# A perceiver layer on one core: the gate product taken in two halves of the tokens, and the threshold search moved ahead

## The chip, the cores and the metric

One core of a Trainium2 chip runs the whole kernel. Its five engines work side by side, each through its own queue in the order written: TensorE (PE, with its weight loads as PEld), VectorE (DVE), ScalarE (ACT), GpSimd (POOL) and SyncE (SP), which here only issues DMA transfers. They meet through semaphores. The metric is the time of one execution in microseconds, the median of several runs. Less is better.

## What is computed

Three residual blocks follow each other on 1024 tokens of width 1024: attention over 16 contexts, a gated feed-forward block whose gate is cut to half, and a mixture of low-rank experts. The change lies in the second.

```python
s = jax.nn.silu(jnp.einsum('bsh,ih->bsi', x, w_gate))       # I = 2752 columns
k = int(0.5 * I)
_, idx = jax.lax.top_k(-jnp.abs(s), k)                      # the k smallest of each row
flat = flat.at[rows, idx.reshape(B * S, k)].set(0.0)        # are set to zero
s = s * jnp.einsum('bsh,ih->bsi', x, w_up)
return jnp.einsum('bsi,hi->bsh', s, w_down)
```

## The kernel before

The tokens are 8 tiles of 128. After attention come four stages, in the function `fast`, which writes the program of every engine out by hand; what an engine does next is what its program says next, and tables of slot numbers put the search beside the products.

**Gate.** The weights come in 8 chunks of 344 columns (`NCH`, `NJ`). SP loads a chunk into the one buffer `g_raw` (1376 KB), POOL rounds it to `g_hi` (L1130) and subtracts to `g_lo` (L1132), and PE multiplies it by all 8 tiles, 24 matmuls each (L1842): the token side is split into `z_hi` and `z_lo` as well. Both halves of the weights have two buffers. Among the first products PE turns the tiles of z (L1825, `turn_z(t+1)` ahead of the product with tile t). ACT rounds them from banks 4 and 5 (L1586), DVE takes their low part (L1236) and normalises the tile after next. ACT takes each product out of one of six banks through Silu into `res` (L1607), and SP stores a chunk to the tensor `s` in memory. `res` lies in the space that the search uses later.

**Search.** For each row the kernel looks for the threshold below which half of |s| lies, on two tiles at a time (a pair). `measure` takes the magnitude of a loaded row tile `mag` and its sum (ACT, L1611). `guess` makes a first cut (DVE, L1268). Then come 7 rounds: DVE counts what lies below the cut in the pair's first tile (L1279), ACT in its second (`compare`, L1617), and DVE works a new cut out of both in eight to ten instructions on two numbers (L1286 to L1308). The seventh round counts both tiles on DVE. Then each tile is finished on DVE by `nearest` (L1316), `best` (L1322), `choose` (L1327 to L1343) and `keep` (L1349), which writes `sx`. SP stores that to `sk` and loads the next `sx` and `mag`. There are three buffers of `mag` and one of `sx`. The semaphore `kept` counts finished tiles.

**Up.** 44 products of 24 matmuls (L1866) run over 22 slices of `w_up_t` (`u_raw`, two buffers, split by POOL in L1139 and L1141); ACT copies each out (L1647), SP stores it to `u_t`. Pairs 0 and 1 are searched whole beside it, and the rounds of pair 2. `ABS_AT`, `ROUNDS_AT`, `MAG_AT` and `SK_AT` name the slots.

**Down.** 66 steps: three groups of tiles (0 to 2, 3 to 5, 6 and 7) times 22 slices. A step turns a slice of `sk` (PE, L1880), multiplies it by `t_u` (DVE, L1374), rounds it (ACT, L1665), takes the low part (DVE `take_low`, L1383), and makes 18 or 12 matmuls (L1897) with slices of `w_down` that POOL splits (L1151, L1153). DVE also finishes tiles 4 to 7 in steps 0 to 7 and 24 to 31 (`FINISH_AT`) and runs the rounds of pair 3 in steps 9 to 21 (`LATE_ROUNDS_AT`).

## Time and profile before

| | us |
|---|---|
| median of 3 runs | 1511.86 (1511.83 to 1512.56) |
| the profiled execution | 1506.71 |
| its span in the trace | 1504.5 |
| gate, up, down of tiles 0 to 5: start in the trace | 607.5, 860.4, 1107.0 |
| steps 44 to 65 of down and the last mixture: start | 1361.0 |

PE is busy for 93% of the span, DVE 67%, POOL 59%, ACT 46%. The mean clock granted to PE is 0.976 of full speed. The span is what the trace's windows add up to; the profiled execution is 2.2 us longer than it.

### The profile page before, as it was taken

How to read it: one execution, taken by the hardware profiler on the slowest of the kernel's cores; microseconds unless marked ns; L12 is line 12 of the kernel's file. 1: busy time of each engine (PE TensorE's matmuls, PEld its weight loads, DVE VectorE, ACT ScalarE, POOL GpSimd, SP SyncE). 2: the span in 40 equal slices, each digit the busy share in tenths (PEclk: the TensorE clock that was granted, in tenths of full speed). 3: DMA queues.
4: the chain of work that ended last, by engine and by line, in shares of the span. 5: the costliest groups of instructions: out<-in, count | busy, mean ns of one | idle time of the engine just before them, and what ended most of it. 6: DMA issues, size and time to landing. Idle time of an engine off the chain costs nothing.

```text
span 1504.5 us, 30249 instructions
## 1 busy us (share of the span) xinstructions
PE 1399.6 (93%) x12775; PEld 1029.4 (68%) x12775; DVE 1010.9 (67%) x1328; ACT 696.8 (46%) x905; POOL 880.8 (59%) x424
## 2 busy tenths in 40 slices
PE   3999999999999999899999999999987888899965
PEld 3555555555555555799999988888865666787843
DVE  7788888888888888810000059897558888655663
ACT  1788888888888888311111152424312320111211
POOL 0699888889888888332242123353245665687830
PEclk9999999999999999999999999999999998999987
DMA  9023433323232330023322373848277756855612
GB/s 334 2 89 108 151 107 129 104 90 103 89 103 90 103 104 2 29 76 109 117 76 76 99 253 94 299 151 284 78 256 263 263 154 215 275 170 172 179 50 86
DMA packets 110320, 208.04 MB, mean 138 GB/s; under 512 B 8080, under 2 KB 83936, under 8 KB 106080
## 3 DMA queue, kind: packets, MB, share of 16 engines
q1 hardware_dynamic: 89072, 183.47, 35.8%
q10 hardware_dynamic: 21104, 22.55, 4.9%
q8 instruction: 102, 1.67, 0.4%
q14 instruction: 42, 0.34, 0.1%
HBM read 163.80 MB, written 42.21 MB: 137 GB/s over the span
## 4 chain that ended last, share of the span: by engine, by line
PE 83%; DVE 10%; issue 4%; ACT 1%; DMA 1%; POOL 0%; DVEq 0%; ACTq 0%; SPq 0%; POOLq 0%
PE fast_psum L1866 16%; PE fast_psum L1842 16%; PE fast_psum L1759 15%; PE fast_psum L1777 14%; PE fast_psum L1897 10%; PE fast_psum L1796 5%; DVE fast_h_lo L1383 2%; PE fast_psum L1803 1%; PE fast_psum L1959 1%; PE fast_psum L1924 1%; PE fast_psum L1782 1%; DVE fast_ln_stats L98 1%; DVE fast_below L1279 1%; PE fast_psum L1880 1%; DMA fast_sx<-s 1%
## 5 line engine op out<-in xcount | busy, mean ns | idle before, releaser
L1209 DVE TENSOR_TENSOR fast_masked<-fast_psum,fast_mask_t 128x1024 f32<-128x1024 f32 (+1 forms) x416 | 488.1, 1218 | 68.7 <-PE fast_psum L1759 67.1
L1098 POOL TENSOR_TENSOR fast_pair<-fast_probs 128x1024 f32<-128x1024 f32 x192 | 457.2, 2384 | 107.4 <-ACT fast_probs L1549 49.2
L1549 ACT ACTIVATE fast_probs<-fast_masked 128x1024 f32<-128x1024 f32 (+1 forms) x416 | 437.5, 1058 | 64.7 <-DVE fast_masked L1209 49.9
L1759 PE MATMUL fast_psum<-fast_qT,fast_kraw 32*128 32x256 f32 (+1 forms) x3328 | 247.3, 403 | 1.5 <-DVE fast_masked L1209 0.8
L1777 PE MATMUL fast_psum<-fast_probs,fast_vraw 128*32 128x256 f32 (+1 forms) x3328 | 226.4, 386 | 0.8 <-ACT fast_probs L1549 0.8
L1759 PEld LDWEIGHTS fast_psum<-fast_qT,fast_kraw 32*128 32x128 f32 (+1 forms) x3328 | 154.1, 182 | 88.5 <-DVE fast_masked L1209 54.8
L1153 POOL TENSOR_TENSOR fast_d_lo<-fast_d_raw,fast_d_hi 128x1024 fp32r<-128x1024 f32 x66 | 164.1, 2487 | 5.3
L1842 PE MATMUL fast_psum<-fast_g_hi,fast_z_hi 128*128 128x344 f32 x512 | 164.8, 322 | 2.6 <-ACT fast_res L1607 2.6
L1842 PE MATMUL fast_psum<-fast_g_lo,fast_z_hi 128*128 128x344 f32 x512 | 163.7, 320 | 0.0
L1842 PE MATMUL fast_psum<-fast_g_hi,fast_z_lo 128*128 128x344 f32 x512 | 163.6, 320 | 0.0
L1268 DVE TENSOR_SCALAR fast_cut<-fast_total 128x2 f32<-128x2 f32 x4 | 0.7, 165 | 239.8 <-ACT fast_mag L1611 239.7
L1777 PEld LDWEIGHTS fast_psum<-fast_probs,fast_vraw 128*32 128x32 f32 (+1 forms) x3328 | 87.1, 109 | 107.0 <-ACT fast_probs L1549 47.5
L1897 PE MATMUL fast_psum<-fast_d_hi,fast_h_hi 128*128 128x512 f32 (+1 forms) x352 | 122.2, 430 | 38.5 <-DVE fast_h_lo L1383 30.1
L1665 ACT CAST fast_h_hi<-fast_t_h 128x384 fp32r<-128x384 f32 (+1 forms) x66 | 31.5, 477 | 266.0 <-DVE fast_t_h L1374 266.0
L1151 POOL CAST fast_d_hi<-fast_d_raw 128x1024 fp32r<-128x1024 f32 x66 | 73.6, 1114 | 119.8 <-PE fast_psum L1897 99.0
L1866 PE MATMUL fast_psum<-fast_z_hi,fast_u_hi 128*128 128x512 f32 (+1 forms) x352 | 139.3, 396 | 0.5 <-ACT fast_res L1607 0.5
L1866 PE MATMUL fast_psum<-fast_z_hi,fast_u_lo 128*128 128x512 f32 (+1 forms) x352 | 139.2, 395 | 0.0
L1866 PE MATMUL fast_psum<-fast_z_lo,fast_u_hi 128*128 128x512 f32 (+1 forms) x352 | 139.2, 395 | 0.0
L1139 POOL CAST fast_u_hi<-fast_u_raw 128x1024 fp32r<-128x1024 f32 (+1 forms) x22 | 25.1, 1142 | 183.1 <-PE fast_psum L1866 102.7
L1796 PE MATMUL fast_psum<-fast_pair,fast_ones 128*32 128x256 f32 x1536 | 118.1, 379 | 1.3 <-POOL fast_pair L1098 1.3
L1607 ACT ACTIVATE fast_res<-fast_psum 128x344 f32<-128x344 f32 x64 | 28.8, 459 | 192.1 <-PE fast_psum L1842 192.1
L1897 PE MATMUL fast_psum<-fast_d_lo,fast_h_hi 128*128 128x512 f32 (+1 forms) x352 | 115.2, 410 | 0.0
(150 smaller groups left out, 2020.5 us busy)
## 6 DMA issues: line engine op xcount, KB each, us to landing
fast_d_raw<-w_down SPq DMA_DIRECT2D x63, 512.0 KB, 3.8
fast_kraw<-ctx_t SPq DMA_DIRECT2D x32, 800.5 KB, 5.9
fast_vraw<-ctx_nat SPq DMA_DIRECT2D x16, 1536.0 KB
fast_g_raw<-w_gate SPq DMA_DIRECT2D x8, 1376.0 KB, 10.3
s<-fast_res SPq DMA_DIRECT2D x8, 1376.0 KB, 6.1
fast_mag<-s SPq DMA_DIRECT2D x8, 1376.0 KB, 10.1
fast_sx<-s SPq DMA_DIRECT2D x8, 1376.0 KB, 6.6
sk<-fast_sx SPq DMA_DIRECT2D x8, 1376.0 KB, 5.4
```

Of the source, the lines that this page charges most:

```text
L1098: pool.tensor_tensor(pair[:, n % PAIR_BUFS], both[:, :, 0, :], both[:, :, 1, :], ALU.add).then_inc(paired, 1)
L1151: pool.tensor_copy(d_hi[j][0:r, :], d_raw[j][0:r, :]).then_inc(d_hi_done, 1)
L1153: pool.tensor_tensor(d_lo[j][0:r, :], d_raw[j][0:r, :], d_hi[j][0:r, :].bitcast(F32), ALU.subtract).then_inc(d_lo_done, 1)
L1209: dve.tensor_tensor(into, of, m, ALU.add).then_inc(mask_added, 1)
L1549: act.activation(probs[0:r, g % RING, hp * HALF:(hp + 1) * HALF], masked[0:r, h % SLOTS, :], ACT.Exp).then_inc(exp_done, 1)
L1665: act.copy(h_hi[n % HS][0:r, 0:w], t_h[n % 2][0:r, 0:w]).then_inc(h_hi_done, 1)
L1759: last = pe.matmul(scores[0:r, (2 * g + hp) % SLOTS, h % 2, i * 256:(i + 1) * 256], kraw[b % BUFS][q, u, c * P:c * P + r], qT[q, b, u, :], ...
L1777: last = pe.matmul(o_acc[q, u, 0:256], vraw[b % BUFS][0:r, c, u * P + h * HD:u * P + (h + 1) * HD], probs[0:r, g % RING, (2 * h + i) * 256 ...
L1796: last = pe.matmul(o_acc[h * HD:(h + 1) * HD, u, 256:512], ones[:, :], pair[:, n % PAIR_BUFS, h, :], start=False, stop=final, skip_group_c ...
L1842: last = pe.matmul(bank[GATE_BANKS[i % GBANKS]][:, 0:NJ], zp[:, k, ts], wp[n % 2][:, k, :], start=(k == 0 and a == 0), stop=(k == DK - 1 a ...
L1866: last = pe.matmul(bank[i % 4][0:r, :], wp[f % 2][:, k, 0:r], zp[:, k, gs], start=(k == 0 and a == 0), stop=(k == DK - 1 and a == 2))
L1897: last = pe.matmul(bank[2 * i + o][:, :], hp[jh][0:r, ts], wp[j][0:r, o * 512:(o + 1) * 512], start=(k == 0 and a == 0), stop=(k == IC - 1 ...
```

## The change

The gate stage now runs over 16 chunks of 4 tiles: all 8 weight chunks with tiles 0 to 3, then the same 8 again with tiles 4 to 7. So each weight chunk is loaded and split twice. `g_raw` has two buffers; the high half is now rounded by ACT (`take_weights`) and only the low half is left to POOL. `res` is half as large and has moved, so the space of the search is free from the ninth chunk on. Pairs 0 and 1 are searched from slot 36 of the 64 gate slots, pairs 2 and 3 beside up, and nothing of the search is left in down.

```diff
+        HT = TILES // 2
+        CHUNKS = 2 * NCH
+        g_raw = [at("g_raw0", WEIGHTS, [DK, NJ]), at("g_raw1", THIN + 2 * HT * NJ, [DK, NJ])]
+        res = [at(f"res{j}", THIN + HT * NJ * j, [HT, NJ]) for j in range(2)]
-        ABS_AT = (0, 1, 13, 14, 27, 28, 38)
-        ROUNDS_AT = (2, 16, 30)
+        GATE_ABS_AT = {36: 0, 37: 1, 44: 2, 54: 3}
+        GATE_ROUNDS_AT = (38, 55)
+        UP_ABS_AT = {4: 4, 5: 5, 12: 6, 19: 7}
+        UP_ROUNDS_AT = (6, 20)
+        UP_SK_AT = {1: 2, 3: 3, 9: 4, 10: 5, 15: 6, 17: 7}
+        UP_MAG_AT = {0: 4, 1: 5, 3: 6, 9: 7}
-        FINISH_AT = {0: 4, 4: 5, 24: 6, 28: 7}
...
+            for c in range(CHUNKS):                       # SP
+                if c + 2 < CHUNKS:
+                    load_gate(c + 2)
...
+                store_gate(c)
+                if c + 1 == NCH:
+                    for j in range(2):
+                        sp.wait_ge(s_stored[j], 16 * (NCH // 2))
+                    for t in range(MAGS):
+                        load_mag(t)
+                    load_sx(0)
...
+            for c in range(1, CHUNKS):                    # POOL
+                j = c % 2
+                if c == 1:
+                    pool.wait_ge(z_ready, TILES)
+                    pool.wait_ge(pv_done, ASTEPS)
+                pool.wait_ge(g_hi_done, c + 1)
+                pool.tensor_tensor(g_lo[j][:, :, :], g_raw[raw(c)][:, :, :], g_hi[j][:, :, :].bitcast(F32),
+                                   ALU.subtract).then_inc(g_lo_done, 1)
...
+            for q in range(HT, SLOTS_G):                  # ACT
+                take_gate(q)
+                if q % HT == 0 and q // HT + 1 < CHUNKS:
+                    take_weights(q // HT + 1)
+                if q in GATE_ABS_AT:
+                    measure(GATE_ABS_AT[q])
+                for p in range(2):
+                    if 0 <= q - GATE_ROUNDS_AT[p] < ROUNDS - 1:
+                        compare(p, q - GATE_ROUNDS_AT[p])
...
+            for q in range(SLOTS_G):                      # PE
+                if q + 1 < TILES:
+                    turn_z(q + 1)
+                gate(q)
```

On ACT the products of a chunk stood in one row at the start of the gate. Before (`res0`, `res1` are the two halves of `res`, the CAST rows round tiles of z):

```order
L115 ACTIVATE fast_ln2_sd<-fast_ln2_mv 128x1
L1586 CAST fast_z_hi_61<-fast_psum 128x4x128 x2
L115 ACTIVATE fast_ln2_sd<-fast_ln2_mv 128x1
L1586 CAST fast_z_hi_61<-fast_psum 128x4x128 x4
L1607 ACT_TABLE_LOAD
L1607 ACTIVATE fast_res0_102<-fast_psum 128x344 x8
```

And after, from the same place of ACT:

```order
L1584 CAST fast_z_hi_61<-fast_psum 128x4x128 x2
L1601 CAST fast_g_hi1_66<-fast_g_raw0_63 128x2752
L115 ACTIVATE fast_ln2_sd<-fast_ln2_mv 128x1
L1584 CAST fast_z_hi_61<-fast_psum 128x4x128 x2
L115 ACTIVATE fast_ln2_sd<-fast_ln2_mv 128x1
L1584 CAST fast_z_hi_61<-fast_psum 128x4x128 x2
L115 ACTIVATE fast_ln2_sd<-fast_ln2_mv 128x1
L1584 CAST fast_z_hi_61<-fast_psum 128x4x128 x2
L1592 ACT_TABLE_LOAD
L1592 ACTIVATE fast_res0_103<-fast_psum 128x344 x4
L1584 CAST fast_z_hi_61<-fast_psum 128x4x128 x2
L1592 ACTIVATE fast_res1_104<-fast_psum 128x344
```

A rounding of weights stands among the tiles of z, and the last tile of z is taken after the first four products.

On SP, where the first half of the gate ends, after (before, the four loads of `mag` and `sx` stood behind the last store of the gate and a load of `u_raw`):

```order
L966 DMA s<-fast_res1_104 128x4x344
L985 DMA fast_mag0_105<-s 128x2752
L985 DMA fast_mag1_106<-s 128x2752
L985 DMA fast_mag2_107<-s 128x2752
L990 DMA fast_sx_111<-s 128x2752
L961 DMA fast_g_raw1_64<-w_gate 128x2752
L966 DMA s<-fast_res0_103 128x4x344
```

A load of gate weights now stands behind the four. 

On DVE, the first steps of down before (`t_h` is the product, `h_lo` its low part, the rest is the finishing of tile 4):

```order
L1374 TENSOR_TENSOR fast_t_h0_118<-fast_psum,fast_t_u0_114 128x384
L1316 SCALAR_TENSOR_TENSOR fast_near_107<-fast_mag1_105,fast_cut 128x2752
L1317 TENSOR_SCALAR fast_rank<-fast_off 128x1
L1374 TENSOR_TENSOR fast_t_h1_119<-fast_psum,fast_t_u1_115 128x384
L1383 TENSOR_TENSOR fast_h_lo0_123<-fast_t_h0_118,fast_h_hi0_120 128x384
L1322 MAX fast_top<-fast_near_107 128x8
L1374 TENSOR_TENSOR fast_t_h0_118<-fast_psum,fast_t_u2_116 128x384
```

And after:

```order
L1383 TENSOR_TENSOR fast_bad<-fast_bad,fast_outside 128x1
L1393 TENSOR_TENSOR fast_t_h0_119<-fast_psum,fast_t_u0_115 128x384
L1393 TENSOR_TENSOR fast_t_h1_120<-fast_psum,fast_t_u1_116 128x384
L1402 TENSOR_TENSOR fast_h_lo0_124<-fast_t_h0_119,fast_h_hi0_121 128x384
L1393 TENSOR_TENSOR fast_t_h0_119<-fast_psum,fast_t_u2_117 128x384
```

Only the steps' own products and low parts are left there.

## Rows read from the trace of the kernel before

**Rows 1.** The page's chain that ended last: share of the span by engine.
```profile
PE 83%; DVE 10%; issue 4%; ACT 1%; DMA 1%; POOL 0%; DVEq 0%; ACTq 0%; SPq 0%; POOLq 0%
```

**Rows 2.** Windows: stretch (us), length, each engine's busy us, PEclk, DMA share, GB/s.
```profile
640.00:860.40 220.40, 219.79 (x1393) 219.54 (x1393) 3.77 (x5) 28.23 (x63) 61.02 (x17) 0.99 0.26 89
860.40:1107.00 246.60, 246.60 (x1058) 196.19 (x1059) 174.87 (x301) 89.37 (x93) 81.07 (x44) 1.00 0.58 195
1107.00:1300.20 193.20, 156.63 (x660) 124.39 (x658) 170.66 (x214) 36.02 (x48) 113.67 (x63) 0.91 0.72 242
1300.20:1358.20 58.00, 58.00 (x272) 47.06 (x271) 26.24 (x50) 8.36 (x17) 47.15 (x26) 1.00 0.63 189
```

**Rows 3.** Waits of PE from 1107 to 1301: total, times, longest.
```profile
PE fast_psum L1897 <- DVE fast_h_lo L1383: 30.1, 12, 3.8
```

**Rows 4.** Chain in order of time, steps 21 to 23 of down: start, length, what.
```profile
1238.07 4.37 PE fast_psum L1897 x18
...
1245.37 6.90 PE fast_psum L1897 x18
...
1252.60 4.13 PE fast_psum L1897 x18
```

**Rows 5.** Timeline at the start of the gate, PE and POOL: start, length, instruction, [idle before].
```profile
627.14 1.04 PE L1825 MATMUL fast_psum<-fast_eye,fast_xres 128*128 128x128 f32 x8
...
633.87 2.49 POOL L1130 CAST fast_g_hi<-fast_g_raw 128x2752 fp32r<-128x2752 f32 x1 [22.07 <-DVE fast_xo L110]
636.43 6.03 POOL L1132 TENSOR_TENSOR fast_g_lo<-fast_g_raw,fast_g_hi 128x2752 fp32r<-128x2752 f32 x1
```

**Rows 6.** PE after a hole in the gate: timeline, and a window of that stretch.
```profile
640.06 0.63 PE L1842 MATMUL fast_psum<-fast_g_hi,fast_z_hi 128*128 128x344 f32 x1 [2.59 <-ACT fast_res L1607]
...
640.00:643.00 3.00, 2.94 (x10) 2.97 (x11) 2.97 (x2) 1.67 (x5) 2.47 (x1) 0.50 0.00 0
```

**Rows 7.** Timeline of ACT: a product taken out of the gate, a magnitude in up.
```profile
754.59 0.46 ACT L1607 ACTIVATE fast_res<-fast_psum 128x344 f32<-128x344 f32 x1 [3.30 <-PE fast_psum L1842]
...
877.10 2.51 ACT L1611 ACTIVATE fast_mag<-fast_mag 128x2752 f32<-128x2752 f32 x1 [0.25 <-DMA fast_mag<-s]
```

**Rows 8.** Transfers: SP and POOL timelines, and a DMA row (KB each, us to landing).
```profile
860.36 0.41 SPq L950 DMA_DIRECT2D s<-fast_res  x1
...
866.61 1.31 SPq L969 DMA_DIRECT2D fast_mag<-s  x3
...
888.23 1.04 POOL L1139 CAST fast_u_hi<-fast_u_raw 128x1024 fp32r<-128x1024 f32 x1 [12.72 <-DMA fast_u_raw<-w_up_t]
...
fast_g_raw<-w_gate SPq DMA_DIRECT2D x4, 1376.0 KB, 9.8
```

**Rows 9.** Timeline of DVE: meetings with POOL, a round, the finishing of a tile.
```profile
638.90 3.72 DVE L1251 TENSOR_SCALAR fast_inside<-fast_rden 128x256 f32<-128x256 f32 x1
...
889.38 2.38 DVE L1306 SCALAR_TENSOR_TENSOR fast_da<-fast_db,fast_da 128x2 f32<-128x2 f32 x1
...
899.01 3.08 DVE L1279 TENSOR_SCALAR_CACHE_REDUCE fast_below<-fast_mag,fast_cut 128x2752 bf16<-128x2752 f32 x1
...
903.89 3.08 DVE L1279 TENSOR_SCALAR_CACHE_REDUCE fast_below<-fast_mag,fast_cut 128x2752 bf16<-128x2752 f32 x1
...
938.92 3.08 DVE L1316 SCALAR_TENSOR_TENSOR fast_near<-fast_mag,fast_cut 128x2752 f32<-128x2752 f32 x1
...
949.95 3.08 DVE L1349 SCALAR_TENSOR_TENSOR fast_sx<-fast_near,fast_thr,fast_sx 128x2752 f32<-128x2752 f32 x1
```

**Rows 10.** Transfers of a finished tile and of up's weights: SP, POOL, a DMA row.
```profile
1028.65 0.32 SPq L978 DMA_DIRECT2D sk<-fast_sx  x1
1033.33 0.33 SPq L974 DMA_DIRECT2D fast_sx<-s  x1
...
1046.84 1.04 POOL L1139 CAST fast_u_hi<-fast_u_raw 128x1024 fp32r<-128x1024 f32 x1 [14.45 <-DMA fast_u_raw<-w_up_t]
...
fast_u_raw<-w_up_t SPq DMA_DIRECT2D x21, 512.0 KB, 6.9
```

More of the change, by code:

```diff
@@ L671, in fast @@
         PAIRS = TILES // 2
+        HT = TILES // 2
+        CHUNKS = 2 * NCH
+        SLOTS_G = CHUNKS * HT
         GROUPS = ((0, 1, 2), (3, 4, 5), (6, 7))
@@ L790, in fast @@
         z_lo_done = sem("z_lo_done")
-        g_full = sem("g_full")
+        g_full = [sem(f"g_full{j}") for j in range(2)]
         g_hi_done = sem("g_hi_done")
@@ L1351, in _ @@
             dve.wait_ge(iota_ready, 1)
-            for p in range(U_PAIRS):
+            for p in range(PAIRS):
                 guess(p)
@@ L1360, in _ @@
                     keep(t)
-            for r in range(ROUNDS):
-                if r == 0:
-                    guess(U_PAIRS)
-                search(U_PAIRS, r)
+            dve.wait_ge(step, steps[0])
+            done(dve.tensor_reduce(good[:, :], settled[:, :], AX.X, ALU.min))
+            dve.wait_ge(step, steps[0])
+            done(dve.tensor_scalar(bad[:, :], good[:, :], -1.0, 1.0, ALU.mult, ALU.add))
+            dve.wait_ge(step, steps[0])
+            dve.tensor_tensor(bad[:, :], bad[:, :], outside[:, :], ALU.add).then_inc(bad_ready, 1)
             def multiply(n):
@@ L1587, in take_z_high, with take_gate, take_weights @@
                          bank[4 + h].rearrange("p (k t) -> p k t", t=P)).then_inc(z_hi_done, 1)
+            def take_gate(q):
+                c, t = divmod(q, HT)
+                if t == 0 and c >= 2:
+                    act.wait_ge(s_stored[c % 2], 16 * (c // 2))
+                act.wait_ge(g_done, q + 1)
+                act.activation(res[c % 2][:, t, :], bank[GATE_BANKS[q % GBANKS]][:, 0:NJ], ACT.Silu).then_inc(g_copied, 1)
+            def take_weights(c):
+                act.wait_ge(g_full[raw(c)], 16 * raw_loads(c))
+                if c == 1:
+                    act.wait_ge(pv_done, ASTEPS)
+                    act.wait_ge(paired, B * (PER - 1))
+                else:
+                    act.wait_ge(g_done, (c - 1) * HT)
+                act.copy(g_hi[c % 2][:, :, :], g_raw[raw(c)][:, :, :]).then_inc(g_hi_done, 1)
             ln2.scalar(act, 0)
@@ L1594, in _ @@
             spread_output(UNITS - 1)
-            for t in range(1, TILES):
+            for t in range(1, TILES - 1):
                 if t + 1 < TILES:
```

168 lines of the change are left out of this document (62 added, 106 removed).

## Prediction

> **What bounds the kernel now.** I read the chain of work that ended last, then the windows by stage, then the waits of the stage that has holes, then the timeline of each engine around the places that the change touches. The chain is PE for 83% of the span and DVE for 10% [rows 1]: PE is the bound nearly everywhere. The windows say where not. In the gate after 640 us PE is busy 219.8 of 220.4 us, in up all of 246.6, in steps 31 to 43 of down all of 58.0. In steps 0 to 30 of down it is busy 156.6 of 193.2 us, at 0.91 of its clock, and DVE 170.7 [rows 2]. PE waits there for the low half that DVE makes, 12 times, 30.1 us in all [rows 3]: DVE has the search between its products. So the gate has nothing to win and everything to lose, and down has a gain with a ceiling.
>
> **What down gives back.** The 13 undisturbed steps take 58.0 us [rows 2], 4.46 each. Steps 0 to 30 at that pace are 138.3 us. The change of group at step 22 stays, since DVE there adds in the residual in both kernels: from the start of step 21 to that of step 23 there are 14.53 us where two steps are 8.92 [rows 4], so 5.6 is kept. Before step 0 the first slice must be turned, multiplied, rounded and subtracted in any case. I take 2.2 us for that, an estimate between nothing and the 5.6 of the change of group, where DVE has more to do. Sum 146.1 against 193.2: **47.1 us saved**. What is late next is PE itself; POOL keeps the pace of the 13 steps with DVE as empty as it will be now, since it is busy 47.2 of 58.0 us there [rows 2].
>
> **Its start costs the gate a hole.** The product with the second chunk was due after 8 tiles and is now due after 4: when PE has turned z tile 5, at 628.2 [rows 5]. Its low half still waits on POOL for all 8 tiles to be normalised, and POOL got that at 633.87 [rows 5]. The tile that comes last hangs on PE's turn at 627.14, which stands ahead of the product that waits, so it isn't late, but no earlier either. ACT has the high half ready before. POOL needs 6.1, so PE starts at 640.1: a hole of 11.9 us. After a hole PE runs at 0.50 of its clock, that is the 1.2 GHz level, for some microseconds [rows 6]; the step after 1245.37 took 6.90 instead of 4.37 [rows 4]. I take 2.3 for such a restart, between 0 and 2.5. Then a second hole: ACT takes z tile 6 after that product, loads its table, takes four products and z tile 7, and only then tile 4's product and chunk 2's weights (2.5, as a magnitude of the same width [rows 7]), then POOL's 6.1. By these lengths chunk 2 is ready 2.4 us late, with a restart. In return the hole of 2.6 at 640.06 [rows 6] and its restart, 2.2, go. Together the second half starts **14 us later**, at 754 instead of 740.
>
> **Steady chunks cost nothing.** A tile takes 0.46 + 3.30 = 3.76 us [rows 7], a chunk 15.0. Its successor's high half starts on ACT 4.3 after the chunk does, takes 2.5, the low half 6.1: 13.2 of 15.0. The cover is thin: 1.8 us. Whatever holds ACT or POOL for longer is a hole in PE.
>
> **The loads at the half.** At 754 SP stores chunk 7 and waits for it to land; the store at 860.36 took until 866.61, 6.3 us [rows 8], one half as large some 4.3. Then come three `mag` and one `sx`, and behind them, on the same queue, the gate weights of chunk 10. In the trace the four loads and 1.5 MB behind them, 7.0 MB, had landed 21.6 us after the first was issued [rows 8]. A load from w_gate alone lands in 9.8 [rows 8], longer than its bytes need at that rate, so chunk 10 lands 26 to 30 us after the half starts; I take 28. ACT wants it at 19.3. Less the cover of 1.8 that is a hole of **7 us** (5 to 9), behind which a restart follows. It also holds ACT, and so both magnitudes of pair 0: the first guess falls at about 790.5.
>
> **Then the search sets the pace of the gate.** ACT does a compare in each of six slots, ahead of the next product and the next weights. A round on DVE takes 4.88 us (899.01 to 903.89 [rows 9]), a slot 3.76. And DVE and POOL shut each other out: DVE's instruction at 638.90, beside POOL's split that ran from 636.43 to 642.46, took until that ended [rows 5, 9]; one at 889.38 on two numbers took 2.38 [rows 9] where it takes 0.16 alone. The counts of 3.08 don't suffer. I follow the chain from 790.5:
> - six rounds 28.5 and the last 6.5; finishing tile 0 takes 14.1 (938.92 to 953.03 [rows 9]): 839.6. Three splits of 6.1 fall on it. One that meets a count first costs what is left of it, about 3.5; one that meets the last round 0.6; one in front of `keep` 4.3. `kept` 1 at 848. Chunk 12's weights come behind the sixth compare: hole of some 6 in PE.
> - `sk` is stored in 4.7 (1028.65 to 1033.33 [rows 10]), and 1.5 for the chunk's store ahead of it; `sx` and `mag` 3 need 10.6, the time of two such loads at the rate above and their start. 865. Magnitude 2.7: second guess at 868.5. Tile 1 is finished by then, barely.
> - five rounds 23.7, the sixth compare 2.7, splits on them 4.8: 899.7. Three products are left: 901.1.
> - up's first weights are loaded only when ACT has taken slot 59, at 890.4. They land in 6.9 to 7.9 [rows 10], and POOL splits them in 3.5: 902.4.
> Up starts at 902.4 instead of 860.4: **42 us lost**. PE's holes at chunks 10, 12 and 15 lie inside that sum and aren't added. Its bounds: 31, if no meeting of DVE and POOL falls on the chain, and 47, if the load and the meetings go to their high ends.
>
> The Trainium skill, "SBUF — State Buffer", section "Who interferes with whom", says that VectorE with two SBUF inputs and a GpSimd instruction that reads SBUF exclude each other for the whole instruction, and its summary advises to schedule what is off the critical path. By this rule every meeting with a 6.1 us split costs up to all of it, and the sum is the 42 above; the trace shows that once, for 3.72 us, and else only meetings with shorter splits. If a meeting cost no more than it did in up, the sum would be 36.
>
> **Up.** It runs 246.6 us of matmuls as before. Its start follows a hole of over 3 us: one restart, 2.3. Then SP is in the way. In slice 1 it waits for `kept` 3 (about 928 by the same rounds) before it may issue the weights of slice 4. In the trace such weights, behind a store, `sx` and `mag`, reached POOL 13.5 us after the `sx` load (1033.33 to 1046.84 [rows 10]). That gives 946.7, split at 950.2, where PE wants them at 949.5: 0.7, call it 1. Later pairs end inside up: DVE is through at about 1100, up at 1152, so nothing of the search reaches down.
>
> **Sum.** 42 + 2.3 + 1 − 47.1 = −1.8 us. The span becomes 1502.7, the profiled execution 1504.9 from 1506.71, and the median of 1511.86, 0.3% above that execution, becomes 1510.0.
>
> **Rivals.**
> - The exclusion is kinder. For it: in up only meetings of 2.4 us or less are seen, and whether a split falls on a count or behind it is luck; against it: 638.90 held for the long split. Half the meetings less is 6.5 us off the chain: 1503.5. With none the loss is 31 and no hole stands before up: 1496.
> - SP makes PE wait in up, and this is the slower side. Cover for slice 4's weights is nil by my sum. Each microsecond by which tile 2 is finished later goes into PE, with a restart. Rounds 5 and 6 of pair 1 and the finishing of tile 2 run while POOL splits up's first slices back to back; three more meetings of 2.4 make 7, the restart 2.3: 1518 to 1519. It decides once `kept` 3 comes later than 928. Against it: in up before the same pattern just held, POOL got the weights at 1046.84 and PE didn't wait [rows 2, 10].
> - The change doesn't clear down: DVE would have to be 50 us late at up's end. I give it nothing.
> - w_gate's load isn't held up: were it served with the `mag` loads and not behind them, hole and chain would lie 5 us earlier, 1505. That lies with the first rival.
>
> **How the numbers follow.** Measuring can tell about 0.2%, 3 us. My forecast, gain and loss within 3 us of each other, has 0.38 and 1507 to 1513 for its own range. Faster by more, the first rival and the load that isn't held: 0.37. Slower by more, the third case and holes that I haven't found, of which a schedule with 1.8 us of cover has room for some: 0.25. For 8 in 10 the range goes from 1500, most of the kinder exclusion, to 1518.
>
> **What the profile should show.** The search is gone from DVE in down, and steps 0 to 30 last 146 us, not 193; a figure above 155 would say that POOL or the loads held it. PE's first product with chunk 1 has 12 us idle before it. A load of `g_raw` lands about 28 us after slot 32 starts, and POOL's split of chunk 10 ends a wait of PE of 5 to 9 us. The next holes are before slots 48 and 60, and up's first matmul is near 902, released by POOL or by the last Silu. DVE's small instructions of 0.16 us show lengths of 3 to 6 where POOL splits gate weights; if none is over 2.4, the first rival holds. PE waits for `u_lo` at up's ninth product by 1 us or so; over 5 is the second rival. I am wrong as a whole if up starts before 893 or after 910.

## The result and the profile after

The changed kernel takes **1500.71 us** (median of 6 executions, 1495.37 to 1502.77) beside 1510.97 for the kernel before (6 executions, 1509.37 to 1512.56). The ratio is 0.9931, with a 95% interval from 0.9914 to 0.9947. So the change gains 10 us, 0.7%. The forecast was 1510.0. The measured time lies near the low end of its range, and the gain is larger than the 0.2% that I had called "no change".

The profiled executions lie closer together: 1506.71 before (span 1504.5) and 1502.54 after (span 1500.8). The stages show where the 3.7 us between those spans come from. First the chain that ended last, from the page of the changed kernel:

```profile
PE 78%; DVE 12%; DMA 3%; ACT 2%; issue 2%; POOL 2%; SPq 0%; DVEq 0%; ACTq 0%; POOLq 0%
```

PE had 83% before [rows 1]. The five points are a difference of two larger moves. In the gate, from 607 us to up's start, PE had some 96% of the chain before and has 37% now, the rest being mostly DVE's and the loads'; in the first 31 steps of down it had 26% and has 90% now. The windows of the changed kernel, of the gate, up, the first steps of down, and the tail (stretch, length, busy us of each engine, PEclk, DMA share, GB/s):

```profile
core 0: us, PE busy (x) PEld busy (x) DVE busy (x) ACT busy (x) POOL busy (x), PEclk, DMA share, GB/s
640.00:901.20 261.20, 237.24 (x1456) 235.77 (x1456) 112.01 (x188) 105.53 (x115) 93.12 (x19) 0.95 0.45 164
901.20:1151.00 249.80, 248.70 (x1062) 197.59 (x1062) 177.87 (x270) 66.64 (x77) 79.73 (x44) 0.99 0.55 184
1151.00:1298.60 147.60, 143.88 (x666) 116.78 (x665) 47.29 (x73) 17.56 (x35) 115.32 (x65) 0.99 0.76 244
1357.00:1500.80 143.80, 113.60 (x536) 85.69 (x536) 76.39 (x177) 23.07 (x54) 68.04 (x39) 0.87 0.37 117
```

Against [rows 2] the gate has gone from 220.4 us, nearly all of them busy, to 261.2 with 24 idle. In the first steps of down DVE's busy time has fallen from 170.7 to 47.3, and PE's granted clock there has risen from 0.91 to 0.99. PE's waits from 600 us on (total, times, longest) have changed sides too:

```profile
PE fast_psum L1860 <- POOL fast_g_lo L1148: 26.9, 5, 11.7
...
PE fast_psum L1883 <- ACT fast_res L1592: 8.2, 1, 8.2
PE fast_psum L1914 <- DVE fast_xin L1410: 4.9, 2, 2.5
...
PE fast_psum L1883 <- POOL fast_u_lo L1158: 1.0, 1, 1.0
```

The 30.1 us for `h_lo` of [rows 3] are gone; 26.9 for the gate's low halves and 8.2 ahead of up have come. The holes one by one, from PE's timeline (start, length, instruction, idle time before it): the fifth gate product, the first with chunk 2, with chunk 10, with chunk 12 and with chunk 15, up's first, and up's ninth product.

```profile
640.63 0.65 PE L1860 MATMUL fast_psum<-fast_g_hi,fast_z_hi 128*128 128x344 f32 x1 [11.72 <-POOL fast_g_lo L1148]
...
661.72 0.51 PE L1860 MATMUL fast_psum<-fast_g_hi,fast_z_hi 128*128 128x344 f32 x1 [2.09 <-POOL fast_g_lo L1148]
...
788.94 0.65 PE L1860 MATMUL fast_psum<-fast_g_hi,fast_z_hi 128*128 128x344 f32 x1 [5.06 <-POOL fast_g_lo L1148]
...
827.63 0.66 PE L1860 MATMUL fast_psum<-fast_g_hi,fast_z_hi 128*128 128x344 f32 x1 [5.58 <-POOL fast_g_lo L1148]
...
877.72 0.43 PE L1860 MATMUL fast_psum<-fast_g_hi,fast_z_hi 128*128 128x344 f32 x1 [2.45 <-POOL fast_g_lo L1148]
...
901.29 0.80 PE L1883 MATMUL fast_psum<-fast_z_hi,fast_u_hi 128*128 128x512 f32 x1 [8.24 <-ACT fast_res L1592]
...
948.71 0.50 PE L1883 MATMUL fast_psum<-fast_z_hi,fast_u_hi 128*128 128x512 f32 x1 [1.01 <-POOL fast_u_lo L1158]
```

Down's turns in the changed kernel: the first two, which stand together, and those ahead of step 31 and of step 43.

```profile
1150.37 0.82 PE L1897 MATMUL fast_psum<-fast_eye,fast_t_sk 128*128 128x128 f32 x6
...
1296.09 0.49 PE L1897 MATMUL fast_psum<-fast_eye,fast_t_sk 128*128 128x128 f32 x3
...
1349.58 0.38 PE L1897 MATMUL fast_psum<-fast_eye,fast_t_sk 128*128 128x128 f32 x2
```

The stages in one table, for the two kernels and for those of the experiments below. The columns are: the start of up's first matmul; the start of down's first turn of `t_sk`; the time from there to the turn that stands ahead of step 43, so the first turns and steps 0 to 42 (the expectations below call this stretch "the 44 steps"; it holds 43); the span of the profiled execution; and the median of the timed ones.

| kernel | up starts | down starts | to step 43 | span | median |
|---|---|---|---|---|---|
| before, three profiles | 860.4 to 861.1 | 1106.9 to 1108.4 | 246.2 to 246.6 | 1503.8 to 1505.8 | 1508.8 of 59 |
| changed, two profiles | 901.3, 900.9 | 1150.4, 1150.0 | 199.2, 199.9 | 1500.8, 1498.8 | 1500.4 of 17 |
| no start wait | 890.2 | 1139.5 | 199.7 | 1488.0 | 1489.65 |
| early load | 893.5 | 1142.6 | 200.0 | 1492.3 | 1493.88 |
| both edits | 883.4 | 1132.5 | 200.2 | 1481.7 | 1483.66 |
| both, ScalarE's places too | 880.8 | 1128.7 | 199.1 | 1477.1 | 1479.50 |
| split in four | 905.1 | 1154.2 | 200.2 | 1504.4 | 1504.10 |
| no search | 882.4 | 1128.8 | 197.9 | 1477.0 | 1478.61, one execution |
| halves alone | 875.2 | 1121.6 | 244.4 | 1517.0 | 1521.79 |
| down cleared, second form | 861.0 | 1108.3 | 203.1 | 1462.8 | 1463.74 |

### The profile page after: what moved, and what is told of

Its sections match the earlier page's. It is cut to its first block, busy times and chain, and to the rows that moved or that the text cites. A ratio compares the mean times of both kernels' runs of the same rounds, so it can differ in the third digit from the quotient of the medians.

```text
span 1500.8 us, 30308 instructions
## 1 busy us (share of the span) xinstructions
PE 1397.6 (93%) x12775; PEld 1030.0 (69%) x12775; DVE 989.9 (66%) x1328; ACT 730.6 (49%) x920; POOL 910.0 (61%) x425
## 4 chain that ended last, share of the span: by engine, by line
PE 78%; DVE 12%; DMA 3%; ACT 2%; issue 2%; POOL 2%; SPq 0%; DVEq 0%; ACTq 0%; POOLq 0%
PE fast_psum L1776 15%; PE fast_psum L1883 15%; PE fast_psum L1914 15%; PE fast_psum L1794 14%; PE fast_psum L1860 7%; PE fast_psum L1813 5%; DVE fast_below L1296 2%; DMA fast_g_raw<-w_gate 1%; PE fast_psum L1976 1%; DVE fast_ln_stats L98 1%; PE fast_psum L1820 1%; POOL fast_g_lo L1148 1%; PE fast_psum L1897 1%; PE fast_psum L1941 1%; PE fast_psum L1799 1%
## 5 line engine op out<-in xcount | busy, mean ns | idle before, releaser
L1148 POOL TENSOR_TENSOR fast_g_lo<-fast_g_raw,fast_g_hi 128x2752 fp32r<-128x2752 f32 x15 | 91.8, 6120 | 173.3 <-ACT fast_g_hi L1601 151.3
L1860 PE MATMUL fast_psum<-fast_g_hi,fast_z_hi 128*128 128x344 f32 x512 | 168.8, 330 | 26.9 <-POOL fast_g_lo L1148 26.9
L1860 PE MATMUL fast_psum<-fast_g_lo,fast_z_hi 128*128 128x344 f32 x512 | 167.1, 326 | 0.0
L1860 PE MATMUL fast_psum<-fast_g_hi,fast_z_lo 128*128 128x344 f32 x512 | 166.7, 326 | 0.0
L1393 DVE TENSOR_TENSOR fast_t_h<-fast_psum,fast_t_u 128x384 f32<-128x384 f32 (+1 forms) x66 | 33.6, 511 | 193.7 <-PE fast_psum L1897 193.1
L1914 PE MATMUL fast_psum<-fast_d_hi,fast_h_hi 128*128 128x512 f32 (+1 forms) x352 | 117.3, 415 | 5.7 <-DVE fast_xin L1410 4.9
L1860 PEld LDWEIGHTS fast_psum<-fast_g_hi,fast_z_hi 128*128 128x128 f32 x512 | 99.6, 194 | 28.3 <-POOL fast_g_lo L1148 28.3
```

The source lines that it names most:

```text
L1148: pool.tensor_tensor(g_lo[j][:, :, :], g_raw[raw(c)][:, :, :], g_hi[j][:, :, :].bitcast(F32), ALU.subtract).then_inc(g_lo_done, 1)
L1860: last = pe.matmul(bank[GATE_BANKS[q % GBANKS]][:, 0:NJ], zp[:, k, ts], wp[c % 2][:, k, :], start=(k == 0 and a == 0), stop=(k == DK - 1 a ...
L1914: last = pe.matmul(bank[2 * i + o][:, :], hp[jh][0:r, ts], wp[j][0:r, o * 512:(o + 1) * 512], start=(k == 0 and a == 0), stop=(k == IC - 1 ...
```

## Experiments

### The changed kernel again

> The changed kernel once more, with nothing edited. My sum was -1.8 us between profiled executions and the first two profiles lie 4.0 us apart (1506.7 before, 1502.5 after), while the medians lie 10.3 us apart (1511.0 and 1500.7). Theory A (the profile of before was one of its shorter executions): the changed kernel's median is again 1500 to 1502 and its profiled execution is as long; with the two halves of the gate and up ending at 1150 to 1152 and down's first steps at 4.4 to 4.5 us each. Theory B (the changed kernel was lucky in its timed runs): a median of 1503 to 1507, the ratio to the kernel before at 0.995 to 0.998.

Measured: median 1500.4 over 11 executions, beside 1509.2 over 22 of the kernel before; ratio 0.9934, interval 0.9915 to 0.9953. The profile puts up's first matmul at 900.9 and the stretch of down to step 43 at 199.9 us. Theory A holds as to the medians: the gain of 9 to 10 us is real, and the changed kernel wasn't lucky.

### The kernel before again, twice

> The kernel before, unedited, for another profile. Its 22 timed executions beside the last batch run from 1502.6 to 1518.1 us with the median at 1509.2, the changed kernel's 11 from 1497.1 to 1503.7. Theory A (the spread is in down, where VectorE and GpSimd meet at the search's operations by chance of a fraction of a microsecond): attention, gate and up end at the same 1107 within 0.5 us, and the window from 1107 to 1300 holds another number of products; its spread is several us. Theory B (the spread is in the restarts of TensorE's clock in the tail and at the start): down's first 31 steps take 193 us within 1, and the tail after up's and down's last product differs.

> The kernel before a third time, for the same question and with the same expectations as the second: by theory A down's first 31 steps differ by several us between the executions (190 to 200), by theory B they are 193 within 1.

Measured: profiled executions of 1507.79 and 1505.88 us. Down to step 43 took 246.2 and 246.4 us beside 246.6 in the first profile, and its first 31 steps 192.8 and 192.9 beside 193.1. Single steps differ by several us (one of them took 12.5, 4.5 and 6.1 us in the second, third and first profile), but the sum doesn't. So theory A falls, as far as three profiles go, and what theory B said of the 31 steps holds. Its other half is small: what follows after that stretch took 151.2, 149.9 and 151.0 us, and down's start lies between 1106.9 and 1108.4. Their spans of 1504.5, 1505.8 and 1503.8 have a mean of 1504.7, while 59 timed executions of the same kernel have a mean span of 1506.6, with a standard deviation of 3.7. I come back to this in the explanation.

### Gate in halves alone

The search is put back where the kernel before has it; the gate keeps its two halves.

```diff
-        GATE_ABS_AT = {36: 0, 37: 1, 44: 2, 54: 3}
-        GATE_ROUNDS_AT = (38, 55)
-        UP_ABS_AT = {4: 4, 5: 5, 12: 6, 19: 7}
-        UP_ROUNDS_AT = (6, 20)
...
+        ABS_AT = (0, 1, 13, 14, 27, 28, 38)
+        ROUNDS_AT = (2, 16, 30)
...
+        FINISH_AT = {0: 4, 4: 5, 24: 6, 28: 7}
```

> One part of the change alone: the gate in two halves, and the search where the kernel before has it (tiles 0 to 3 and the rounds of 4 and 5 beside up, the rest in down). Theory A (the parts add: 21.5 us for the halves, as the run without a search showed, and nothing else moves): the holes of 11.7, 2.1 and about 5 us, up's first matmul at 882, up 246 to 248 us long, and down's first 31 steps 193 us as in the kernel before; the median at 1530 to 1534 beside about 1510 of the kernel before. Rival B (the halves cost less or more once the search's transfers of mag and sx no longer stand ahead of chunk 10's weights: the hole of 5 us there is the transfers'): up's first matmul at 876 to 878, the median at 1525 to 1528.

Measured: 1521.79 us over 10 executions beside 1508.41 (ratio 1.0081, 1.0058 to 1.0103). Up starts at 875.2, 7 us earlier than theory A said and 1 earlier than rival B. PE's waits and its first matmul in up:

```profile
PE fast_psum L1931 <- DVE fast_h_lo L1398: 28.7, 9, 7.9
...
PE fast_psum L1877 <- POOL fast_g_lo L1146: 13.8, 2, 11.7
...
875.16 0.50 PE L1900 MATMUL fast_psum<-fast_z_hi,fast_u_hi 128*128 128x512 f32 x1 [0.55 <-ACT fast_res L1609]
```

There are only two holes, 11.7 and 2.1 us. There is none at chunk 10: with no `mag` and no `sx` in the queue its weights come in time. Nor is there one later: 16 chunks in place of 8 cost nothing while ScalarE and GpSimd have nothing else to do. The halves alone put up's start 14.8 us later. Down is much as in the kernel before (244.4 us for 246.2 to 246.6). The median came out 3 us below rival B's 1525 and 8 below A's 1530.

### No search

The changed kernel without VectorE's rounds and finishing and without ScalarE's comparisons: `sk` is a plain copy of `s`, and every transfer stays. It ran once.

```diff
             for p in range(PAIRS):
                 guess(p)
-                for r in range(ROUNDS):
-                    search(p, r)
-                for t in (2 * p, 2 * p + 1):
-                    nearest(t)
-                    best(t)
-                    choose(t)
-                    keep(t)
+                for t in (2 * p, 2 * p + 1):
+                    dve.wait_ge(sx_full, 16 * (t + 1))
+                    dve.tensor_scalar(settled[:, t:t + 1], total[:, t:t + 1], 0.0, 1.0, ALU.mult, ALU.add).then_inc(kept, 1)
...
-                for p in range(2):
-                    if 0 <= q - GATE_ROUNDS_AT[p] < ROUNDS - 1:
-                        compare(p, q - GATE_ROUNDS_AT[p])
...
```

> The changed kernel with the search left out: VectorE's rounds and its finding and masking of the largest values, and ScalarE's comparing, so that sk is a copy of s and each tile is marked as kept as soon as its values are loaded; every transfer, ScalarE's sums of the magnitudes, and the splits stay. It prices the gate in two halves alone. Theory A (the holes ahead of chunks 12 and 15 and 7 of the 8 us ahead of up come from the search beside the second half): they are gone or, ahead of chunk 15, where the store of s and a load share the transfers, at most 3.7; the holes of 11.7, 2.1 and 5 us stay; up's first matmul at 887 to 890, so 27 to 30 of the 41 us by which up is later than before are the halves', and 12 to 14 the search's. Rival B (the holes are those of the split beside the loads and would be there without a search): up's first matmul at 898 or later.

Measured, in PE's waits over the whole span and its timeline:

```profile
PE fast_psum L1851 <- POOL fast_g_lo L1148: 18.7, 3, 11.7
...
882.35 0.50 PE L1874 MATMUL fast_psum<-fast_z_hi,fast_u_hi 128*128 128x512 f32 x1 [0.55 <-ACT fast_res L1589]
```

Three holes are left: 11.7, 2.1 and 4.9 (chunk 10). Those ahead of chunks 12 and 15 and of up are gone. Theory A holds as to the holes and rival B falls, but its price was off: up starts 5 us earlier than it said, so the search costs 18.9 us and not 12 to 14. The hole ahead of chunk 15 is the search's too, and not the store's. Beside halves alone this gives three prices: 14.8 us for the halves, 7.2 for the loads of `mag` and `sx` ahead of chunk 10, and 18.9 for the search beside the second half.

### GpSimd's wait at the start taken out

```diff
                 if c == 1:
-                    pool.wait_ge(z_ready, TILES)
                     pool.wait_ge(pv_done, ASTEPS)
```

> The changed kernel without GpSimd's wait for all eight normalised tiles ahead of the low split of chunk 1. Theory A (that wait makes the 11.7 us hole ahead of the fifth gate product): the hole is gone or under 3 us, the hole ahead of chunk 2 grows from 2.1 to about 3.7, the second half starts about 7 us earlier (747 for 754), up's first matmul 6 to 8 us earlier (894 for 901.3), since all behind it hangs on it. Rival B (the split only moves onto VectorE's normalising of tiles 4 to 7, which then makes the products late): a hole of about as much ahead of slots 4 to 7, up's first matmul at 899 to 902, no change in the time.

Measured: 1489.65 us (ratio to the kernel before 0.9873, 0.9841 to 0.9904), 10.8 us under the changed kernel. GpSimd's first two splits, and PE's first product with chunk 2, in this kernel:

```profile
623.71 6.07 POOL L1147 TENSOR_TENSOR fast_g_lo<-fast_g_raw,fast_g_hi 128x2752 fp32r<-128x2752 f32 x1 [11.40 <-ACT fast_g_hi L1600]
646.32 6.07 POOL L1147 TENSOR_TENSOR fast_g_lo<-fast_g_raw,fast_g_hi 128x2752 fp32r<-128x2752 f32 x1 [16.54 <-ACT fast_g_hi L1600]
...
652.45 0.43 PE L1859 MATMUL fast_psum<-fast_g_hi,fast_z_hi 128*128 128x344 f32 x1 [2.09 <-POOL fast_g_lo L1147]
```

The split stands at 623.7 in place of 634.6. What it pushes back among VectorE's normalisations shows as one hole of 3.3 us ahead of a turn of z; rival B's price is that, not 11.7:

```profile
631.08 1.73 PE L1841 MATMUL fast_psum<-fast_eye,fast_xres 128*128 128x128 f32 x7 [3.26 <-DVE fast_z_lo L1252]
```

The hole ahead of chunk 2 hasn't grown to 3.7, as theory A had it: it is 2.09 as before. The second half of the gate starts 10.8 us earlier and up 11.1, more than the 7 I gave them. The two holes account for 8.5 of that. Of the rest, 1.7 is a restart that is gone behind chunk 2's hole (5.6 us at 0.70 of the clock). The windows after the hole ahead of chunk 2 show it, first in the changed kernel:

```profile
661.40:667.00 5.60, 5.28 (x24) 5.28 (x25) 0.00 (x0) 0.00 (x0) 0.27 (x1) 0.70 1.01 351
```

PE is granted 0.70 here, and 0.70 to 0.71 in the same stretch of the changed kernel's second profile, early load and no search, which kept the wait. After the same hole of 2.09 us the kernel without the start's wait is granted 1.00:

```profile
652.40:657.00 4.60, 4.55 (x29) 4.56 (x30) 0.00 (x0) 0.41 (x2) 0.00 (x0) 1.00 1.04 352
```

What decides between the two isn't shown. A hole some 20 us back alone doesn't: both kernels have one, of 11.7 us in the first and 3.3 in the second, and both run at 0.50 right behind it.

### Chunk 10's weights ahead of mag and sx

```diff
-                if c + 2 < CHUNKS:
+                if c + 2 < CHUNKS and c != NCH:
                     load_gate(c + 2)
...
                 if c + 1 == NCH:
+                    load_gate(NCH + 2)
                     for j in range(2):
```

> The changed kernel with chunk 10's gate weights loaded ahead of the three loads of mag and the one of sx, not behind them. Theory A (the shared transfers put chunk 10's weights 26 us behind the start of the half, and so make the 5.1 us hole, and hold mag's tiles 0 and 1 back): the hole ahead of chunk 10 is gone, the first guess comes at once or up to 7 us later than 788 by the larger queue ahead of mag, up's first matmul 5 to 9 us earlier than 901.3 (the loads' order costs the search nothing: it starts when ScalarE's two sums are through, which stand behind chunk 10's high half on ScalarE). Rival B (the search is what bounds the second half, and its first guess is set by mag's loads): up's first matmul within 2 us of 901.3, with the holes ahead of chunks 12 and 15 and of up larger by what chunk 10's lost.

Measured: 1493.88 us (ratio 0.9899, 0.9870 to 0.9928), 6.5 us under the changed kernel. SP's queue at the half, ScalarE's high half of chunk 10, and the first guess on VectorE, in the changed kernel:

```profile
757.74 1.29 SPq L985 DMA_DIRECT2D fast_mag<-s  x3
759.07 0.85 SPq L990 DMA_DIRECT2D fast_sx<-s  x1
759.96 0.47 SPq L961 DMA_DIRECT2D fast_g_raw<-w_gate  x1
...
780.27 2.49 ACT L1601 CAST fast_g_hi<-fast_g_raw 128x2752 fp32r<-128x2752 f32 x1 [7.12 <-DMA fast_g_raw<-w_gate]
...
788.20 0.71 DVE L1285 TENSOR_SCALAR fast_cut<-fast_total 128x2 f32<-128x2 f32 x1 [133.10 <-ACT fast_mag L1623]
```

The same with the load moved ahead:

```profile
754.38 0.51 SPq L961 DMA_DIRECT2D fast_g_raw<-w_gate  x1
757.93 1.43 SPq L985 DMA_DIRECT2D fast_mag<-s  x3
...
772.68 2.49 ACT L1602 CAST fast_g_hi<-fast_g_raw 128x2752 fp32r<-128x2752 f32 x1
...
780.62 0.86 DVE L1286 TENSOR_SCALAR fast_cut<-fast_total 128x2 f32<-128x2 f32 x1 [125.85 <-ACT fast_mag L1624]
```

Theory A holds. ScalarE has chunk 10 7.6 us earlier and without waiting, the hole is gone, and the guess, which stands behind chunk 10 on ScalarE and not behind the loads of `mag`, comes 7.6 us earlier too. Up starts 7.4 to 7.8 us earlier. By this, 7 us of the changed kernel's 41 are the order of five transfers.

### GpSimd's split in four pieces

```diff
-                pool.tensor_tensor(g_lo[j][:, :, :], g_raw[raw(c)][:, :, :], g_hi[j][:, :, :].bitcast(F32),
-                                   ALU.subtract).then_inc(g_lo_done, 1)
+                for q in range(4):
+                    ks = slice(q * DK // 4, (q + 1) * DK // 4)
+                    last = pool.tensor_tensor(g_lo[j][:, ks, :], g_raw[raw(c)][:, ks, :], g_hi[j][:, ks, :].bitcast(F32),
+                                              ALU.subtract)
+                last.then_inc(g_lo_done, 1)
```

> The changed kernel with GpSimd's low split of each gate chunk cut into four instructions of a quarter each (four times about 1.5 us for one of 6.0). Theory A (VectorE's instructions of two SBUF operands wait out a whole instruction of GpSimd, and GpSimd waits out VectorE's: the exclusion costs what both want together): the single long VectorE instructions (7.4 us for a keep of 3.1, 6.0 and 3.4 us for ones of 0.2) are gone, none over 4.7 us, but GpSimd's split as a whole gets longer beside a search, because it is let in piece by piece, so up's first matmul moves by no more than 3 us either way (898 to 905). Rival B (only the long meeting itself costs): up's first matmul 5 to 8 us earlier, 893 to 896.

First what is to be taken apart, in the changed kernel. Four of VectorE's instructions beside GpSimd's splits, the first two beside the one from 798.74 to 804.92:

```profile
797.87 3.08 DVE L1296 TENSOR_SCALAR_CACHE_REDUCE fast_below<-fast_mag,fast_cut 128x2752 bf16<-128x2752 f32 x1
...
801.46 3.47 DVE L1311 TENSOR_TENSOR fast_db<-fast_cut 128x2 f32<-128x2 f32 x1
...
838.60 7.38 DVE L1366 SCALAR_TENSOR_TENSOR fast_sx<-fast_near,fast_thr,fast_sx 128x2752 f32<-128x2752 f32 x1
...
852.19 5.95 DVE L1344 TENSOR_SCALAR fast_hit<-fast_iota,fast_rank 128x8 f32<-128x8 f32 x1
...
836.93 6.17 POOL L1148 TENSOR_TENSOR fast_g_lo<-fast_g_raw,fast_g_hi 128x2752 fp32r<-128x2752 f32 x1 [9.35 <-ACT fast_g_hi L1601]
851.97 6.15 POOL L1148 TENSOR_TENSOR fast_g_lo<-fast_g_raw,fast_g_hi 128x2752 fp32r<-128x2752 f32 x1 [8.87 <-ACT fast_g_hi L1601]
```

The count keeps its 3.08 us. The instruction on two numbers at 801.46 ends with the split. `keep` starts at 838.60 and ends at 845.98, where its own work is 3.1 us: it waited until GpSimd was through at 843.10. The comparison of eight numbers at 852.19 ends with GpSimd's split, at 858.1. With the split in four (GpSimd's rows group the four pieces):

```profile
840.26 4.25 DVE L1369 SCALAR_TENSOR_TENSOR fast_sx<-fast_near,fast_thr,fast_sx 128x2752 f32<-128x2752 f32 x1
844.55 4.38 DVE L1336 SCALAR_TENSOR_TENSOR fast_near<-fast_mag,fast_cut 128x2752 f32<-128x2752 f32 x1
...
838.31 12.12 POOL L1150 TENSOR_TENSOR fast_g_lo<-fast_g_raw,fast_g_hi 128x688 fp32r<-128x688 f32 x4 [9.06 <-ACT fast_g_hi L1604]
859.09 9.33 POOL L1150 TENSOR_TENSOR fast_g_lo<-fast_g_raw,fast_g_hi 128x688 fp32r<-128x688 f32 x4 [8.66 <-ACT fast_g_hi L1604]
```

VectorE's longest is 4.38 us, but GpSimd's split now takes 12.1 and 9.3 us for 6.15, and new holes of 3.9 and 1.1 us stand ahead of chunks 13 and 14. Up starts at 905.1, 4 us later, and the kernel takes 1504.1 us, 3.7 us more. Undisturbed, the four pieces take 6.4 to 6.6 us together, so most of the rest is waiting. Rival B falls, and theory A's bound of 3 us was 1 too small. Here smaller pieces passed the waiting on to GpSimd.

### Both edits together

> The changed kernel with both edits: GpSimd's low split of chunk 1 does not wait for the eight normalised tiles, and chunk 10's weights are loaded ahead of mag and sx. Alone they gave 10.8 us and 6.5 us against the changed kernel's 1500.4. Theory A (the two holes lie one behind the other, in the first half and in the second, and each moves all that follows): the gains add, up's first matmul at 883 (901.3 less 11.1 less 7.4), the median at 1482 to 1485. Rival B (both take the idle time out from under the same search, which then sets the end of the second half): the gain of the two together is no more than 13 us, the median 1487 to 1490.

Measured: **1483.66 us** (ratio 0.9823, 0.9805 to 0.9842), 16.7 us under the changed kernel; up's first matmul at 883.41. Theory A holds, to 0.6 us: 10.8 and 6.5 add up to 17.3.

### And ScalarE's comparisons placed by the time of a round

```diff
-        GATE_ABS_AT = {36: 0, 37: 1, 44: 2, 54: 3}
-        GATE_ROUNDS_AT = (38, 55)
+        GATE_ABS_AT = {33: 0, 36: 1, 47: 2, 52: 3}
+        GATE_COMPARE_AT = ((37, 37, 39, 40, 40, 43), (53, 55, 57, 57, 59, 60))
...
-                    if 0 <= q - GATE_ROUNDS_AT[p] < ROUNDS - 1:
-                        compare(p, q - GATE_ROUNDS_AT[p])
+                    for r in range(ROUNDS - 1):
+                        if GATE_COMPARE_AT[p][r] == q:
+                            compare(p, r)
```

> The kernel with both edits, and ScalarE's part of the first two searches placed by the time each round takes (rounds of pair 0 behind products 37, 37, 39, 40, 40, 43, of pair 1 behind 53, 55, 57, 57, 59, 60; the sum of tile 2 at 47, of tile 3 at 52, of tiles 0 and 1 at 33 and 36), so that the high halves of chunks 12 and 15 do not stand behind a comparison that waits for a cut. Theory A (the holes ahead of chunk 12 and of up, 6.3 and 6.7 us in the kernel with both edits, are ScalarE held by its comparisons): the hole ahead of chunk 12 falls to about 3, that ahead of up to under 1, that ahead of chunk 15 grows from 2.4 to about 7, up ends 5 us earlier, the median at 1478 to 1480 for 1483.7. Rival B (what is lost is set by VectorE's and GpSimd's time, whatever ScalarE does): the holes only change places, the median at 1483 to 1485.

Measured: **1479.50 us** (ratio 0.9795, 0.9767 to 0.9823). The holes ahead of chunks 12 and 15, and of up:

```profile
810.31 0.42 PE L1861 MATMUL fast_psum<-fast_g_hi,fast_z_hi 128*128 128x344 f32 x1 [1.10 <-POOL fast_g_lo L1148]
...
862.96 0.65 PE L1861 MATMUL fast_psum<-fast_g_hi,fast_z_hi 128*128 128x344 f32 x1 [7.27 <-POOL fast_g_lo L1148]
...
880.80 0.50 PE L1884 MATMUL fast_psum<-fast_z_hi,fast_u_hi 128*128 128x512 f32 x1 [0.55 <-ACT fast_res L1592]
```

Theory A holds, with a hole of 3.5 at chunk 11 that it didn't name. Beside both edits alone down starts 3.8 us earlier, for the 5 it gave, and the median is 4.2 us lower. This is the fastest kernel of the study: 21 us under the changed kernel and 29 under the one before.

### Down cleared of the search

In the kernel before, the search is left out of down alone: the `sk` of tiles 4 to 7 is a plain copy of `s`.

```diff
-                    if n == at_step:
-                        nearest(t)
-                    if n == at_step + 1:
-                        best(t)
-                    if n == at_step + 2:
-                        choose(t)
                     if n == at_step + 3:
-                        keep(t)
+                        dve.wait_ge(sx_full, 16 * (t + 1))
+                        dve.tensor_scalar(settled[:, t:t + 1], total[:, t:t + 1], 0.0, 1.0, ALU.mult,
+                                          ALU.add).then_inc(kept, 1)
...
-                if 0 <= r < ROUNDS and off_beat == 0:
-                    search(PAIRS - 1, r)
...
```

> The kernel before with the search left out of down alone: the picking and masking of tiles 4 to 7 and the rounds of tiles 6 and 7 (VectorE's and ScalarE's), so that those tiles' sk is a copy of s; their transfers and ScalarE's sum of magnitudes stay. Theory A (down's first 31 steps are bound by those instructions and are worth 47.1 us without them, as steps 31 to 43 are): the steps at 4.4 to 4.5 us, the 31 of them 146 to 148 us, the median 45 to 48 us under that of the kernel before (1461 to 1464). On the spread of the executions (a standard deviation of 3.5 us over 31 of the kernel before, 2.2 over 17 of the changed one, 0.8 over 5 of the one with both edits): if it is down's stalls, after which TensorE's clock is granted at half by chance, that make the spread, it falls to under 2 us here; if not, it stays at 3 or more.

Measured: 1479.97 us, only 28 us under the kernel before. Steps 0 to 30 took 158.9 us, where 146 to 148 were expected. Both theories missed what my own edit did, which VectorE's and SP's timelines show:

```profile
1152.54 0.15 DVE L1472 TENSOR_SCALAR fast_settled<-fast_total 128x1 f32<-128x1 f32 x1 [15.20 <-DMA fast_sx<-s]
...
1141.42 0.33 SPq L974 DMA_DIRECT2D fast_sx<-s  x1
```

VectorE comes to the mark of tile 5 before its `sx` is even loaded, and the products queue behind it. The work I had taken out had been the cover of a transfer. The second form moves these marks and the transfers around them:

```diff
-        LATE_SK_AT = {5: 4, 9: 5, 28: 6, 32: 7}
-        LATE_SX_AT = {7: 5, 11: 6, 30: 7}
-        LATE_MAG_AT, LATE_ABS_AT, LATE_ROUNDS_AT = 6, 8, 9
+        LATE_SK_AT = {5: 4, 13: 5, 28: 6, 36: 7}
+        LATE_SX_AT = {7: 5, 15: 6, 30: 7}
+        LATE_MAG_AT, LATE_ABS_AT, LATE_ROUNDS_AT = 6, 8, 16
...
-        FINISH_AT = {0: 4, 4: 5, 24: 6, 28: 7}
+        FINISH_AT = {0: 4, 9: 5, 24: 6, 31: 7}
```

> The kernel before with the search left out of down alone, as in the run before this one (sk of tiles 4 to 7 is a copy of s), but with the marks of tiles 5 and 7 and the loads and stores of sx put later, since there VectorE waited 15.2 and 9.6 us for a load of sx, which the search had hidden, and so made two new holes (steps of 17.5 and 9.9 us). Theory A (down's search costs what its steps show): the 44 steps of down take 199 to 201 us for 246.4, as in the changed kernel, and the median is 45 to 48 us under that of the kernel before. Rival B (part of the gain in the changed kernel's down is due to transfers of mag, sx and sk being gone from it, which here stay): 203 to 215 us. On the spread: under 2 us if the search in down makes it.

Measured: 1463.74 us beside 1508.83 (ratio 0.9685, 0.9658 to 0.9713), 45.1 us less. PE's waits from 1100 to 1360 us:

```profile
PE fast_psum L1888 <- DVE fast_xin L1391: 4.9, 2, 2.5
PE fast_psum L1888 <- DVE fast_h_lo L1383: 1.9, 1, 1.9
```

The stretch to step 43 takes 203.1 us, 3 to 4 more than in the changed kernel, of which one late mark (a step of 6.6 us) is 2. That is outside theory A's 199 to 201 and just inside rival B's 203 to 215, so some 2 us of what down gains in the changed kernel, or 4 with the late mark, may be due to the transfers that are gone from it. The median's gain lies in theory A's range. On the spread of executions see below.

## Why the prediction came out as it did

**Down: right.** Predicted 47.1 us saved and 146 us for steps 0 to 30. From the first turn of `t_sk` to the one ahead of step 43 there are 246.6 us before and 199.2 after, 47.4 less; at the turn that follows step 30 the stretch is 145.7 us. Of the 5.6 us kept for the change of group, 4.6 stayed (13.55 us between two turns that are 8.92 apart elsewhere). Clearing down alone gave 45 us in the median.

**The start of the gate: right.** Predicted a hole of 11.9 us, then one of 2.4, and the second half 14 us late. The holes are 11.72 and 2.09, and the halves alone cost 14.8. That the split's wait was the cause was shown by taking it out.

**Steady chunks: right.** Halves alone has no hole between 663 us and up.

**The loads at the half: mechanism right, 2 us too dear.** I had chunk 10 land 28 us after the half starts, with a hole of 7. It landed at 26, with a hole of 5.06; the low ends of both my intervals. The first guess came at 788.2 for 790.5.

**The search beside the gate: right.** `kept` 1 was due at 848 and came at 845.98; the second pair's first count, due at 868.5, came at 866.1; the last Silu, due at 901.1, released up at 901.3. The holes are where they were announced, ahead of chunk 12 (5.6 us for "some 6"), of chunk 15 and of up. What released up was the last Silu; up's first weights were split at 896.5 and not at 902.4, so the last line of that list was not the last in fact. Its own terms, 6.9 to 7.9 and 3.5 from 890.4, give 900.8 to 901.8 and not 902.4. No search prices all of this at 18.9 us.

**The exclusion: right.** By "SBUF — State Buffer", section "Who interferes with whom", of the Trainium skill, VectorE with two SBUF inputs and a GpSimd instruction that reads SBUF shut each other out for the whole instruction. The trace agrees beside splits of 6.15: 7.38 us for 3.1 at `keep`, and 3.47 us at 801.46 for an instruction on two numbers, both with two tensors in SBUF. The comparison at 852.19 reads one tensor and one number per partition, and took 5.95 us all the same. The split in four shows the other half of the rule, that GpSimd waits in its turn. The first rival, that meetings are cheap, falls. By the median alone it would have seemed right, since 1500.7 lies between its two figures, 1503.5 and 1496; up's start and the lengths in the trace say that it isn't.

**Up: right.** Predicted 2.3 for the restart and 1 for slice 4. Up's first matmul to down's first turn took 249.1 us for 246.5, and the wait for `u_lo` at its ninth product is 1.01 us. The second rival, SP making PE wait in up, didn't come about.

**So the sum of the stages**, put at −1.8 us, is 40.9 + 2.6 − 47.4 = −3.9 in the profiles. The difference of 2.1 us is 1.1 at up's start, 0.7 in up and 0.3 in down.

**The step that failed is the last one**, "and the median of 1511.86, 0.3% above that execution, becomes 1510.0". I carried the 5 us by which one profiled execution lay under the median over to the changed kernel, as if it were part of every kernel. It isn't. The changed kernel's profiled execution was 1.8 us above its median. The 1511.86 was itself a median of three only, 3 us above the 1508.8 of the 59 later executions. That 1500.71 still lies in the range from 1500 on, by 0.7 us, is in part luck: no term of the sum led there. Over all batches the kernel before has a mean span of 1506.6 us (59 timed executions, standard deviation 3.7), the changed kernel 1497.8 (17, standard deviation 2.2): 8.8 us apart, where the profiles' means, 1504.7 of three and 1499.8 of two, are 4.9 apart. Another 0.9 us lies outside the span, where the kernel before spends 3.2 us in the mean and the changed one 2.2.

**What stays open** is whether those last 4 us are sampling or real. With such deviations the difference of three and two single profiles has a standard error of 2.6 us, so 4 is no proof of anything. For a real effect speaks that the two kernels with the search in down spread more (3.7 and 2.8 us) than those without (0.8 to 2.7; 2.1 for down cleared, second form), and that their four profiles lie 2 us under the mean of their timed spans, where the other kernels' lie 1 above. The step from 2.8 to 2.7 is no step, though. It would fit executions in which down's stalls fall worse than in any profile here. No profile shows one, so it isn't shown. That the kernels with an undivided gate spend 1 us or more outside the span beyond what the others do (3.1 to 3.8 us for 1.9 to 2.3) was measured and not explained.

**The chances.** I gave 0.37 to faster by over 0.2%. With a standard deviation of 3.7 us between executions, the distance between a profiled execution and the median should have been in the range from the start, as a term of its own.

## What to carry to other kernels

Don't add the distance between one profiled execution and the median to another kernel's forecast: state the difference between profiles, and let the spread of the executions widen the range. Where work is moved beside another stage, look first at what it does to the queues: of the 41 us that the gate lost here, 11 were one wait written for the order of before and 7 the order of five loads, and both came back with an edit of a line or two each. Work that is taken out may have been the cover of a transfer, so look for what waits in its place.
